# An attention and mixture-of-experts block on one core: padded rough scores, sums kept in PSUM, transposes by DMA, and new engine orders

## The reference

```python
xn = _layernorm(x, axis=-1)
s = attention(xn)     # 32 query heads, 16 key heads of 64, causal, ALiBi bias, softmax, @ W_out
g = _silu(moe(xn))    # 8 experts of width 512, the best 2 by gate logits, exact gelu
x = x + s * g

scores = jnp.einsum('bhqd,bhkd->bhqk', q, k) / math.sqrt(HEAD_DIM) + bias[None]
scores = jnp.where(causal[None, None], scores, -jnp.inf)
attn = jax.nn.softmax(scores, axis=-1)
out = jnp.einsum('bhqk,bhkd->bhqd', attn, v)
```

## Time and profile before

| | |
|---|---|
| three runs | 1368.47 us median (1368.12 to 1368.83) |
| profiled execution, its own time | 1373.28 us |
| its span | 1370.9 us |
| TensorE busy, weight loads | 1251.3 us (91%), 934.0 us (68%) |
| VectorE busy | 1103.1 us (80%) |
| ScalarE busy | 891.0 us (65%) |
| GpSimd busy | 833.9 us (61%) |
| DMA on the hardware queue | 103.18 MB, 30.0% of 16 engines |

### The profile page before, as it was taken

How to read it: one execution, slowest core, us unless ns; L and a number is a source line. 1 busy time by engine, 2 the same in 40 slices (tenths; PEclk the granted TensorE clock), 3 DMA queues, 4 the chain that set the end, 5 groups by cost and what they waited for, 6 DMA issues and landing times.

```text
span 1370.9 us, 53673 instructions
## 1 busy us (share of the span) xinstructions
PE 1251.3 (91%) x18202; PEld 934.0 (68%) x18203; DVE 1103.1 (80%) x3404; ACT 891.0 (65%) x1663; POOL 833.9 (61%) x1015
## 2 busy tenths in 40 slices
PE   1589999999999999988999799999999999999992
PEld 0357677777777777767888477766767777667762
DVE  8778788888888888856888688888888888878864
ACT  1367677777777777765666477667666666666662
POOL 7147677777777777780000177776666676666773
PEclk9789999999999999998999899999999999999996
DMA  7223333333333333322222233333333232333322
GB/s 263 89 64 90 77 86 87 87 89 86 84 84 84 84 84 84 84 64 66 80 80 73 70 79 79 78 77 72 71 75 74 69 73 70 72 74 77 77 55 65
DMA packets 113023, 112.37 MB, mean 82 GB/s; under 512 B 17250, under 2 KB 101570, under 8 KB 112324
## 3 DMA queue, kind: packets, MB, share of 16 engines
q1 hardware_dynamic: 108868, 103.18, 30.0%
q0 software_dynamic: 4096, 8.40, 2.0%
HBM read 18.91 MB, written 16.78 MB: 26 GB/s over the span
## 4 chain that ended last, share of the span: by engine, by line
PE 29%; POOL 14%; issue 6%; DVE 5%; ACT 1%; DVEq 0%; POOLq 0%; DMA 0%; SPq 0%; ACTq 0%
POOL h L609 10%; PE ps L631 4%; PE ps L632 4%; PE ps L633 4%; POOL y_now L601 3%; DVE stage L1112 2%; PE ps L728 2%; PE ps L703 2%; PE outs L759 2%; PE ps L732 1%; PE outs L631 1%; PE outs L632 1%; PE outs L633 1%; PE ps L772 1%; DVE mix L1181 1%
## 5 line engine op out<-in xcount | busy, mean ns | idle before, releaser
L609 POOL TENSOR_TENSOR h<-stage 128x512 f16<-128x512 f32 x640 | 646.2, 1038 | 422.1 <-ACT stage L961 384.6
L1112 DVE CUSTOM_DVE_ANT_0 stage<-ps,kmask 128x512 f32<-128x512 f32 (+3 forms) x1024 | 451.7, 488 | 138.4 <-PE ps L703 136.8
L961 ACT ACTIVATE stage<-ps,slope 128x512 f32<-128x512 f32 (+1 forms) x768 | 432.5, 616 | 84.7 <-PE ps L735 81.2
L728 PE MATMUL ps<-q_st,k_st 128*128 128x256 f16 (+3 forms) x1024 | 303.3, 302 | 7.2 <-ACT stage L961 6.3
L759 PE MATMUL outs<-v_sp,stage 128*128 128x65 f16 x2560 | 292.7, 195 | 15.6 <-POOL h L609 12.1
L950 ACT CAST q_st<-ps 1x512 f16<-1x512 f32 x256 | 147.9, 578 | 219.9 <-PE ps L711 218.4
L761 PE MATMUL outs<-v_sp,stage 128*128 128x64 f16 x2560 | 289.8, 194 | 0.0
L763 PE MATMUL outs<-v_sp,h 128*128 128x65 f16 x2560 | 288.9, 193 | 0.0
L759 PEld LDWEIGHTS outs<-v_sp,stage 128*128 128x128 bf16 x2560 | 234.5, 98 | 70.1 <-POOL h L609 33.2
L761 PEld LDWEIGHTS outs<-v_sp,stage 128*128 128x128 bf16 x2560 | 237.5, 98 | 0.0
L763 PEld LDWEIGHTS outs<-v_sp,h 128*128 128x128 f16 x2560 | 237.4, 99 | 0.0
(11 more groups left out here) (192 smaller groups left out, 2852.3 us busy)
## 6 DMA issues: line engine op xcount, KB each, us to landing
q_st<-q_raw SPq DMA_DIRECT2D x256, 128.0 KB, 2.4
k_st<-k_raw SPq DMA_DIRECT2D x128, 128.0 KB, 2.2
q_st<-q_raw SPq DMA_DIRECT2D x256, 64.0 KB, 2.0
k_st<-k_raw SPq DMA_DIRECT2D x128, 64.0 KB, 2.0
stage<-slot_x SPq DMA_DIRECT2D x40, 128.0 KB, 2.0
slot_y<-stage SPq DMA_DIRECT2D x40, 128.0 KB, 1.7
slot_x<-att SPq DMA_DIRECT2D x2, 2048.0 KB, 8.7
wx_raw<-in_L_ffn_w SPq DMA_DIRECT2D x64, 64.0 KB, 1.8
```

The lines of the kernel that those rows point to most:

```text
L609: pool.tensor_tensor(t_lo[r], t_p[r], upper(t_p[r]), ALU.subtract).then_inc(s[f"lo{u % NG}"], 1)
L728: pe.matmul(d, k[:, 0, at], q[:, 0, seen], start=True, stop=False, skip_group_check=True)
L961: e = act.activation(t_p[r][:, c0:c1], S_ps[u % 2][:, c0:c1], ACT.Exp, scale=slope[:, bass.ds(pair_index(n) * 2 * SLOTS + sl * 2 + h, 1)])
L1112: ins = dve.tensor_tensor_reduce(junk[h][:, c0:c0 + w], M_ps[h][:, c0:c0 + w], kmask[:, SEQ - w:SEQ], 1.0, -3e38, ALU.add, ALU.max, mx[sl] ...
```

## The change

1. **Rough scores.** `k_st` gets two more planes of 512 columns. Plane 2 has the keys on rows 0 to 63 and zeros below, plane 3 zeros above and the keys on rows 64 to 127. Each head's rough scores are a matmul over all 128 rows, a step of its own (`M0` to `M11`), with hand-over between TensorE and VectorE per head. SP issues three DMAs per slot for the keys, not two. GpSimd zeroes the planes once at the start.
2. **One shift row.** Both heads' shifts go to row 64 of `q_st`. The late matmul covers the last 66 columns for both heads.
3. **Normalised in PSUM.** `N` writes the product back into `outs`. `A` is then: ScalarE copies the high part out of `outs` into `a16`, VectorE the rest, SP issues one transposing DMA per slot (1024 columns of fp16) into `aT`, which is kept twice. TensorE's transposes go. `outs` is free for the next slot only after VectorE's part of `A`. The projection of a body stands two windows after it, and each half has one more window at its end.
4. **Fetches.** Index tile and fetched rows exist twice (`slot_now`, `y_now`). The first expert's product moves to ScalarE (`F0`).
5. **Orders.** Each half has its own `ORDER` and `G_USERS`. `q_raw` and `k_raw` move into the space of the staged weights, so ScalarE waits for the split of the value weights before its first projections.

```diff
 def rough(n, par, j):
-    sl, r = divmod(j, NR)
+    sl, r, h = round_of(j)
     need(pe, f"qh{sl}", n + 1)
-    need(pe, f"kst{sl}", (n + 1) * 32)
-    if r == 0:
+    need(pe, f"kst{sl}", (n + 1) * 48)
+    if r > 0:
+        need(pe, f"peak{sl}{h}", n * NR + r)
+    elif h == 0:
         need(pe, f"crow{1 - sl}", n + sl)
     else:
-        need(pe, f"peak{j - 1}", n + 1)
+        need(pe, f"peak{1 - sl}{h}", (n + sl) * NR)
     for i, c0 in ROUNDS[r]:
         w = (i + 1) * P
-        for h in range(2):
-            head = slice(DH * h, DH * h + DH)
-            mm = pe.matmul(M_ps[h][:, c0:c0 + w], q_raw[sl][head, 0, i * P:(i + 1) * P],
-                           k_st[par][sl][head, 0, 0:w], start=True, stop=True)
-    mm.then_inc(s[f"rough{j}"], 1)
+        mm = pe.matmul(M_ps[h][:, c0:c0 + w], q_raw[sl][:, 0, i * P:(i + 1) * P],
+                       k_st[par][sl][:, 2 + h, 0:w], start=True, stop=True)
+    mm.then_inc(s[f"rough{sl}{h}"], 1)
...
+                hi, to = raw[:, 0, :], k_st[par][sl]
+                sp.dma_start(to[DH:2 * DH, 0:4:3, :], hi.unsqueeze(1).to_broadcast([DH, 2, SEQ]))
+                sp.dma_start(to[0:DH, 2, :], hi)
...
+            def turn_out(n, par, sl):
+                sp.wait_ge(s[f"al{sl}"], n + 1)
+                need(sp, "op", n - 1)
+                sp.dma_start_transpose(aT[par][sl].rearrange("p (t q) -> p t q", q=P), a16[sl])
...
 def normalise(n, _, sl):
     group_done(dve, "valued", n, sl * NG + NG - 1)
-    need(dve, f"ta{sl}", n)
...
-    dve.tensor_tensor(a_sb[sl][:, :, :].rearrange("p t (h d) -> p h t d", h=2),
-                      o[:, :, :, OUT_COL[sl]:OUT_COL[sl] + DH],
-                      rden[:, sl, :, :].unsqueeze(3).to_broadcast([P, 2, QT, DH]), ALU.mult)
+    v = values_of(sl)
+    dve.tensor_tensor(v, v, rden[:, sl, :, :].unsqueeze(3).to_broadcast([P, 2, QT, DH]), ALU.mult)
...
 def values(n, par, u):
     if r == 0:
-        need(pe, f"nrm{1 - sl}", n + sl)
+        need(pe, f"al{1 - sl}", n + sl)
...
 def fetch_ready(n, par, k):
-    need(pool, f"added{k}", t)
-    indices(t, k)
+    need(pool, f"added{k}", t - 1)
+    indices(t, k, par)
...
-        ("S0", 0), ("M5", 0), ("P6", -1), ("P7", -1), ("S1", 0), ("P8", -1), ("C1", 0), ("P9", -1), ("S2", 0),
+            ("K0", 1), ("P2", -1), ("C0", 0), ("P3", -1), ("P4", -1), ("S7", -1), ("S8", -1), ("M6", 0), ("M7", 0),
+            ("Q0", 1), ("S9", -1), ("M8", 0), ("M9", 0), ("S0", 0), ("P5", -1), ("P6", -1), ("M10", 0), ("P7", -1),
```

More of the change, by code:

```diff
@@ L49 @@
 G_USERS = [
-    [("Q1", 1), ("A1", -1), ("O0", -1), ("K0", 2), ("A0", 0)],
-    [("V0", 1), ("Q0", 2)],
-]
-ORDER = {
[5 rows of a table removed]
[L61 to L78, removed]
+    [
+        [("K0", 1), ("Q1", 1)],
+        [("Q0", 1), ("O0", -2), ("V0", 1)],
+    ],
@@ new lines @@
+    [
+        [("O0", -2), ("V0", 1)],
+        [("K0", 1), ("Q0", 1), ("Q1", 1)],
+    ],
+]
+ORDER = [
+    {
[6 rows of a table added]
+        ],
+        "ACT": [
+            ("E4", -1), ("E5", -1), ("V0", 0), ("E6", -1), ("K0", 1), ("C0", 0), ("E7", -1), ("A0", -1), ("E8", -1),
+            ("Q0", 1), ("E9", -1), ("E0", 0), ("W0", -1), ("E1", 0), ("C1", 0), ("E2", 0), ("A1", -1), ("E3", 0),
+            ("Q1", 1),
+        ],
+        "DVE": [
[3 rows of a table added]
+        ],
+        "POOL": [
+            ("L6", -2), ("L7", -2), ("L8", -2), ("L9", -2), ("I0", -1), ("I1", -1), ("L0", -1), ("L1", -1),
+            ("L2", -1), ("D0", -1), ("L3", -1), ("L4", -1), ("D1", -1), ("L5", -1),
+        ],
+        "SP": [
+            ("Q0", 1), ("A1", -1), ("K0", 2), ("Q1", 1), ("A0", 0), ("K1", 2), ("W0", 1),
+        ],
+    },
+    {
[6 rows of a table added]
+        ],
+        "ACT": [
+            ("E5", 0), ("V0", 1), ("E6", 0), ("K0", 2), ("C0", 1), ("E7", 0), ("A0", 0), ("E8", 0), ("E9", 0),
+            ("E0", 1), ("F0", 2), ("Q0", 2), ("E1", 1), ("C1", 1), ("A1", 0), ("E2", 1), ("E3", 1), ("Q1", 2),
+            ("E4", 1),
+        ],
+        "DVE": [
[3 rows of a table added]
+        ],
+        "POOL": [
+            ("L6", -2), ("I1", 1), ("D0", 1), ("L7", -2), ("L8", -2), ("L9", -2), ("D1", 1), ("L0", -1), ("L1", -1),
+            ("L2", -1), ("I0", 2), ("L3", -1), ("L4", -1), ("L5", -1),
+        ],
+        "SP": [
+            ("A1", -1), ("K0", 2), ("Q1", 1), ("A0", 0), ("K1", 2), ("Q0", 2),
+        ],
+    },
+]
@@ L236, in build @@
         for step in ("rough", "peak"):
-            for j in range(SLOTS * NR):
+            for j in ("00", "01", "10", "11"):
                 s[f"{step}{j}"] = sem(f"s_{step}{j}")
@@ L290, in run_bodies @@
                     one_window(engine_name, tasks, i_ * UNROLL + c, lo, hi, c)
-            for w in range(end, hi + 1):
+            for w in range(end, hi + 2):
                 one_window(engine_name, tasks, w, lo, hi, w)
@@ L448, in _ @@
             sp.wait_ge(s["sent"], 2 * NT * 16)
+            for sl in range(SLOTS):
+                sp.wait_ge(s[f"ta{sl}"], HALF * 16)
             for b in range(4):
@@ L506, in _ @@
             pool.tensor_copy(ident16[:, :], ident[:, :]).then_inc(s["rows"], 1)
+            for par in range(2):
+                for sl in range(SLOTS):
+                    pool.memset(k_st[par][sl][:, 2:4, :], 0.0)
             pool.memset(late_k[:, :], HIDE_K).then_inc(s["rows"], 1)
@@ L816, in _ @@
                 group_done(pe, "exp", HALF - 1, u)
-            for j in range(SLOTS * NR):
-                pe.wait_ge(s[f"peak{j}"], HALF)
+            for j in ("00", "01", "10", "11"):
+                pe.wait_ge(s[f"peak{j}"], HALF * NR)
             for sl in range(SLOTS):
@@ L972, in _ @@
             act.wait_ge(s["scales"], HQ)
+            act.wait_ge(s["wloP"], len(ON_POOL))
             go_ahead("ACT", tasks, 0, HALF)
```

208 lines of the change are left out of this document (105 added, 103 removed), and 20 rows, old and new, of the table ORDER.

## The result

The changed kernel takes 1432.61 us median (1423.24 to 1435.11, 4 runs), the kernel before 1368.3 us beside it. The ratio is 1.0457, with a 95% interval of 1.0409 to 1.0505: **slower**, where 1276 us was forecast. The profiled execution took 1434.18 us (span 1432.3).

The account below looks back on a forecast made before the run. TensorE's work was taken as the bound, plus GpSimd's chain in the second half. Periods falling from 16.86 to 15.7 and 17.89 to 15.9 us save 37 + 64, less 9 for edges: 92 us, so 1276 us, range 1245 to 1330.

Parts of the forecast that it names:

- VectorE's work, 14.3 us per body: VectorE's busy time per body, said to stay hidden under a 15.7 us period with 1.4 us to spare.
- the three: The rival outcomes: SP's queue as bound (chance 0.16), VectorE as bound (0.17), gaps around rough rounds staying (0.05).
- SP's queue (T): Time one transposing DMA holds SP's queue: taken as 2 us, costing nothing under 3.2 us of first-half room.
- the forecast's edges: Each half ends one window later, with a last DMA transpose: 4.5 us each, +9 us in all.
- Rival 1: SP's queue becomes the bound if a transpose holds it over 3.2 us; 1472 us at 5 us; chance 0.16.
- Rival 2: VectorE becomes the bound, with 0.6 us per body unhidden: 1315 us; chance 0.17.
- Rough scores and late matmuls: TensorE's work per body: 128-row rough matmuls without gaps save 0.04 us, narrower late matmuls 0.08 us.
- The product into PSUM: VectorE's normalising product, 691 ns into SBUF, now writes PSUM: between 0 and +0.3 us each, hidden.
- GpSimd's fetches: Second half: double copies remove GpSimd waits of 1.3 us per body, more than the 1.03 us to be won.
- The sum: First half 37 us saved, second 64, edges 9 lost: 92 us less, a median of 1276 us; chance 0.62.

Follow-up runs that it names:

- the version at 1286.79 us: Changed kernel with tile starts read from PSUM, expert's addition and weights' low part on GpSimd, GpSimd's DMA issues side by side again: 1286.79 us.
- the last version in the table: Changed kernel with tile starts read from PSUM, and the second expert's addition and the expert weights' low part moved to GpSimd: 1306.83 us.
- the version of it with one operand: Kernel before, with the shift reading one SBUF operand and the tile starts put into a longer mask: 1454.54 us, ratio 1.0049.
- the two runs meant to tell: Kernel before with GpSimd's two sends apart, after low parts L1 and L3: 1364.94 us; kernel before with expert weights loaded behind the first queries: 1590.8 us.

## Why the prediction was wrong

- **The step that failed: VectorE's work, 14.3 us per body, carried over at the old durations.** The prediction said that instruction counts on VectorE are as before, and so that it had 1.4 us per body to spare. Counts held. The durations did not: the shift went from 41 us in all (128 at a mean of 318 ns) to 168 us (mean 1309), because GpSimd's new list put a send and two low parts beside it. TensorE waited 105.9 us for it over the run, and ran at the half clock behind some of these waits (mean granted clock 0.953, 0.968 in the kernel before). The forecast had no term for one engine's instruction that lengthens while another works. The signs were in the trace of the kernel before: 193 ns at best and 1096 at worst for one shape.
- The Trainium skill, "SBUF — State Buffer", sections SBUF: two separate sides and Who interferes with whom, has a rule for it. VectorE and GpSimd share a pair of SBUF ports as an exclusive lock, which the one that starts first keeps for its whole instruction while the other is blocked. A VectorE instruction with two SBUF inputs contends in this way with a GpSimd instruction that reads SBUF, and so does one in a mode that uses both ports. The runs agree on the first: 191 ns at the median with one input from PSUM, 850 with both in SBUF. The held instructions with one SBUF input would fit the second, but no trace shows their mode. By that rule this was a rival, and it was not among the three. The page has the loser blocked while the other's instruction lasts; here it was blocked over several.
- **SP's queue (T).** Taken at 2 us. The transposes' queue time (min/median/max), and issue to landing:

```profile
L483 SPq DMA_TRANSPOSE h_hi<-stage x64: 1223/1246/2205, 93.1 to 1397.6; - x64
L483 SPq DMA_TRANSPOSE h_lo<-stage x64: 1232/1251/2034, 108.7 to 1409.3; - x64
```

```profile
h_hi<-stage SPq DMA_TRANSPOSE x64, 3.1
```

  1.25 us, under the 3.2 us of room, and they land 3.1 us after issue. Right in sign. The projections waited for one 9.2 us in all, in two waits of 4.6 us at the ends of the two halves, where the forecast's edges had 4.5 each. Rival 1, the SP queue as the bound, is out. The Trainium skill, "VectorE: DVE Perf Modes", section The three transpose paths, has 1309 ns for one block; eight blocks took 1.25 us of the queue and 3.1 us to landing, so its figure is no price of queue time here.
- **Rival 2, VectorE as the bound**, names the right engine and the wrong reason. In the version at 1286.79 us VectorE is busy 317 and 336 us in 400, and line 1228, once per body there, has starts 16.0 us apart in the first half and 16.1 in the second, on average. Its ordinary work was hidden, as the forecast had it.
- **Rough scores and late matmuls were sized rightly.** From start to next start, over two bodies of the second half of the last version in the table (1000.60 to 1033.17), the 128-row rough matmuls take 4.62 us, 2.31 per body: 2.20 was forecast. In the kernel before (401.53 to 435.25) they take 3.45 us, and in front of each of the twelve rounds the matmul ahead takes some 0.09 us longer than it does elsewhere, 1.13 in all: 2.29 per body, where the forecast had 2.24. So the padding costs 0.02 us per body and not -0.04, which is nothing. The late matmuls, without those gaps, go from 1.27 to 1.07 us: 0.10 per body, where 0.08 was forecast.
- **The product into PSUM** (line 1225): 699 ns against 691. The forecast's 0 to 0.3 us held at its lower end.

```profile
L1225 DVE TENSOR_TENSOR outs<-outs,rden 128x512 f32<-128x512 f32 x44 | 30.8, 699 | 1.5
```

- **GpSimd's fetches.** Of the 37.1 us of the earlier trace rows, from 800 to 1300 us, the wait for VectorE is gone and 2.0 us of the wait for the index copy are left, as forecast.
- **The sum.** 32 x (18.25 - 15.7) + 32 x (18.66 - 15.9) = 170 us, the 153 us between forecast and profiled execution and more; the first bodies are shorter than these averages. On one chip the shift's hold is 67.7 us of what was missed and the other two instructions 35.9. With those three out of the way the kernel is at 1306.83, still 31 us over the forecast of 1276. With GpSimd's old order of sends as well it stands at 1286.8, 11 us over the forecast and inside its range. That is another kernel than the one forecast, with the work of two instructions moved off VectorE, so that it comes near is no proof of the sum. What does hold there is what the forecast said of the parts: TensorE is busy 96.9% and 99.5% (over 97 was forecast for both halves), value matmuls wait 0.3 us for GpSimd after 800 us, and the bodies are 0.3 and 0.2 us longer than forecast.

## What to carry to other kernels

Where VectorE and GpSimd both work, list VectorE's instructions whose operands all lie in SBUF, and look at their min, median and max for one shape. A spread such as 193 to 1096 ns can be a hold: look at what GpSimd does beside the long ones. A new order can move it onto the path, and curing one can leave the next one held. Here the small one right in front of TensorE was worth the most: let one operand come from PSUM, or give it to an engine that has room. Before an order is judged, run it on more than one chip.

## What the runs showed of the hardware

- **The hold outlasts single instructions of GpSimd.** The shift at 372.30 waited through the rest of a send and two low parts. The first began after the shift did, so GpSimd was served first. In the changed kernel 89 shifts took over 0.4 us, and 73 of them outlasted at least one GpSimd instruction that began after them.
- **With one input from PSUM the shift is not held**, though the other is in SBUF: 189 to 197 ns in 128 cases. The reductions of 512 columns with PSUM and SBUF inputs also keep 687 ns (689 before).
- **The kernel before has two speeds.** Its first half has a gap in each body in its one trace from the three jobs of 1453 to 1465 us, and the version of it with one operand, in another of them, has the same. Waits, 200 to 600 us, of the kernel before in such a job:

```profile
ACT q_st L950 <- remote: 47.1, 19, 2.9
PE ps L703 <- ACT q_st L950: 39.8, 19, 2.5
DVE rden L1158 <- remote: 37.6, 19, 2.0
```

  ScalarE and VectorE both wait for steps of TensorE whose rows end some 2 us earlier. The page's word "remote" is a releaser that the profile does not show. TensorE then stands up to 2.5 us in front of line 703, and the granted clock of the stretch is 0.92 where it is 1.00 in the earlier trace rows. The changed kernel's profiles show no such wait, but the version with its old order of GpSimd's sends does. All three traces with these waits have the two sends of a body side by side, and in the two of them looked at the signals are late beside the sends. In the same jobs the versions with the sends apart have none. In the job of the result and in the last one, kernels with the sends side by side have none either. So the sends side by side are part of it and do not suffice. What delays the signals, and why in some jobs alone, stays open: the two runs meant to tell landed on a chip that does not show it. The sign of this change hangs on it: 4.6% slower where the kernel before runs at 1368 us, a ratio of 0.972 in both jobs where it runs at 1454 to 1465. The versions without held instructions beat the kernel before in either kind of job (1306.83 beside 1454.24, 1286.79 beside 1369.63).
